# Second convolution of a pair placed behind the first of the next pair, and sixteen images as two written-out halves

## The chip, the core and the metric

The kernel runs on one core of one Trainium2 chip. The metric is the device time of one execution in microseconds (us), median of the runs shown. The core has five engines that run their own instruction streams and meet at semaphores: TensorE (PE, matmuls), VectorE (DVE), ScalarE (ACT), GpSimd (POOL) and SyncE (SP), which here only issues DMAs, in order.

## The reference, cut to what matters

Sixteen images of 64 channels and 64x64 pixels, float32. All sizes that the kernel works on follow from this:

```
# layer 0
y = leaky_relu(conv2d_3x3(x, conv_w1, conv_b1))
y = leaky_relu(conv2d_3x3(y, conv_w2, conv_b2))
seq = mamba(y as [16, 4096 tokens, 64], ...)      # state scan over 4096 tokens, 128 channels x 16 states
# layer 1, x = result of layer 0
out_c = channel attention(x)                      # 64x64 scores, softmax
out_s = softmax(q k^T over 4096x4096 tokens) v    # q, k of 32 channels
return x + w_bn @ concat(out_c, out_s)
```

The second convolution of an image needs the whole result of its first one, row by row with one row of overlap. The images are independent of each other everywhere.

## The kernel before, in words

There are two phases with barriers between.

**The convolutions** (`convolutions`, line 267). Images go in 8 pairs. A convolution of a pair is 8 chunks of 512 pixels, made as 4 "duos" of two chunks; a duo is 24 matmuls (lines 369 and 376) into two of the 8 PSUM banks. ACT adds the bias (line 388) and DVE makes the leaky ReLU: after the first convolution it writes into `ypad` (lines 404 and 407), after the second into `seq` (line 414). The 3x3 taps want a second copy of each image on the other 64 partitions, shifted by one row. For the input the copy is a second load (lines 313 and 314, into `xpad`); for the first convolution's result it is a DMA from `ypad` to `ypad` (lines 335 and 337, the "moves"). Both tiles exist twice, for even and odd pairs. The order on every engine is pair by pair: first convolution, then second. SP's order in a pair is: 16 loads of the next pair's input, 16 moves of this pair, 8 stores of `seq`. PE waits before a duo of the first convolution for its loads (`loaded`) and before a duo of the second for the moves of the chunks that it reads (`moved`):

```
for k in ((0, 1, 2) if j == 0 else range(2 * j + 1, min(2 * j + 3, CHUNKS))):
    pe.wait_ge(moved[par][k], 32 * (p // 2 + 1))
```

**The pipeline** (`pipeline`, line 419). Time is cut in ticks, 128 to an image and 16 to a chunk. In one tick all stages of several images are worked on: the scan of the current image (DVE line 1152, POOL line 1269, fed by the `lanes` DMAs of line 720 three ticks ahead), and the attention of the image before (PE lines 899, 901, 911, 926 and 836; ACT line 1007). `Span(j, images, tail)` lays out the ticks of consecutive images, and `span(...)` writes them out as one block of straight code per engine. A span begins at a tick where the neighbouring images' work is half done, so nothing of the computation is drained or repeated at a joint between spans. But the block ends: SP waits until every DMA of the span has landed (line 813), the engines meet at a barrier (line 264), GpSimd clears all semaphores one by one (line 263), and a second barrier follows. The spans are images 0 to 2 written out, then a hardware loop of three rounds with four images written out in its body (images 3 to 6, 7 to 10, 11 to 14), then image 15. That makes four joints: into the loop, two at its back edge, and out of it. In the loop the image number is a register, from which SP makes the DRAM addresses.

Of the kernel before, what the change touches and what calls it, by code (L numbers as in the profile page):

```python
# [23 lines left out]
P = 128  # L24
IMAGES, CH, HH, WW = 16, 64, 64, 64
L = HH * WW
PAIRS = IMAGES // 2
# [23 lines left out]
SEARCH = -6  # L51
TURN = SEARCH + KT + 1
QUERY_LOAD = SEARCH - 3
LOOPED = 4
END = 14
KEY_LOAD = [MAIN - KT + 8 * (p + 1) + 1 for p in range(QUARTERS)]
SEARCH_LOAD = [SEARCH - KT + 8 * (p + 1) + 1 for p in range(QUARTERS - 1)] + [GROUPS]
# [17 lines left out]
PAIRED = CHUNKS // 2  # L75


SPANS = ((0, 3, 0), (3, LOOPED, 0), (IMAGES - 1, 1, MAIN + TICKS + END + 1))
assert (IMAGES - 1 - 3) % LOOPED == 0 and NT * PAIRED == KT


def shape_constants():
# [181 lines left out]
    nc.all_engine_barrier()  # L264


def convolutions(nc, banks, x, w1, b1, w2, b2, seq_d):


# [2 lines left out]
    with ExitStack() as ctx:  # L272
# [20 lines left out]
        with nc.Block() as block:  # L293
# [10 lines left out]
            @block.sync  # L304
            def _(sp):
                def load_pair(p):

                    par = p % 2
                    for j in range(DUOS):
                        a, b = ROWS_OF[j:j + 2]  # L310
                        for i in range(2):
                            img = x[p, CH * i:CH * (i + 1), a:b, :]
                            sp.dma_start(xpad[par][i][0:CH, 1 + a:1 + b, 1:1 + WW], img).then_inc(loaded[par][j], 16)
                            sp.dma_start(xpad[par][i][CH:P, a:b, 1:1 + WW], img).then_inc(loaded[par][j], 16)

                for t, w, b, col in ((wtap[0], w1, b1, 0), (wtap[1], w2, b2, 1)):
                    sp.dma_start(t[0:CH, 0:3, :], w[:, 0:3, :]).then_inc(weights, 16)
                    sp.dma_start(t[CH:P, 0:3, :], w[:, 3:6, :]).then_inc(weights, 16)
                    for half in (0, CH):
                        sp.dma_start(t[half:half + CH, 3:6, :], w[:, 6:9, :]).then_inc(weights, 16)  # L320
                        sp.dma_start(bias[half:half + CH, col:col + 1], b).then_inc(weights, 16)
                sp.wait_ge(edged, 2)
                load_pair(0)
                for p in range(PAIRS):
                    par = p % 2
                    if p + 1 < PAIRS:
                        if p == 0:
                            sp.wait_ge(edged, 8)
                        else:
                            sp.wait_ge(summed, 2 * DUOS * (p - 1) + DUOS)  # L330
                        load_pair(p + 1)
                    for k in range(CHUNKS):
                        sp.wait_ge(leaky, 2 * CHUNKS * p + k + 1)
                        low, high = slice(1 + k * ROWS, 1 + (k + 1) * ROWS), slice(k * ROWS, (k + 1) * ROWS)
                        sp.dma_start(ypad[par][0][CH:P, high, 1:1 + WW],
                                     ypad[par][0][0:CH, low, 1:1 + WW]).then_inc(moved[par][k], 16)
                        sp.dma_start(ypad[par][1][0:CH, low, 1:1 + WW],
                                     ypad[par][1][CH:P, high, 1:1 + WW]).then_inc(moved[par][k], 16)
                    for k in range(CHUNKS):
                        sp.wait_ge(leaky, 2 * CHUNKS * p + CHUNKS + k + 1)  # L340
                        sp.dma_start(seq_d[2 * p:2 * p + 2].rearrange("a c l -> (a c) l")
                                     [:, k * CHUNK:(k + 1) * CHUNK], seq[:, k % 2, :]).then_inc(stored[k % 2], 16)
                for s in stored:
                    sp.wait_ge(s, 16 * PAIRS * CHUNKS // 2)

            @block.tensor
            def _(pe):
                pe.wait_ge(weights, 12 * 16)
                for p in range(PAIRS):
                    par = p % 2  # L350
                    for conv in range(2):
                        src = (xpad, ypad)[conv][par]
                        for j in range(DUOS):
                            first = 2 * CHUNKS * p + CHUNKS * conv + 2 * j
                            if first >= 8:
                                pe.wait_ge(plus_bias, first - 6)
                            if conv:

                                for k in ((0, 1, 2) if j == 0 else range(2 * j + 1, min(2 * j + 3, CHUNKS))):
                                    pe.wait_ge(moved[par][k], 32 * (p // 2 + 1))  # L360
                            else:
                                pe.wait_ge(loaded[par][j], 64 * (p // 2 + 1))
                            into = [[banks[(first + h) % 8][CH * i:CH * (i + 1), :].rearrange("p (h w) -> p h w", w=WW)
                                     for i in range(2)] for h in range(2)]
                            for h in range(2):
                                top = (2 * j + h) * ROWS
                                for dx in range(3):
                                    for i in range(2):
                                        nc.tensor.matmul(into[h][i], wtap[conv][:, dx, :],
                                                         src[i][:, top:top + ROWS, dx:dx + WW],  # L370
                                                         start=dx == 0, stop=False)
                            for dx in range(3):
                                for h in range(2):
                                    o, top = CH * h, (2 * j + h) * ROWS + 2 - h
                                    for i in range(2):
                                        mm = nc.tensor.matmul(into[h][i], wtap[conv][o:o + CH, 3 + dx, :],  # L376
                                                              src[i][o:o + CH, top:top + ROWS, dx:dx + WW],
                                                              start=False, stop=dx == 2, tile_position=(o, CH * i))
                            mm.then_inc(summed, 1)

            @block.scalar
            def _(act):
                for n in range(2 * CHUNKS * PAIRS):
                    conv = n // CHUNKS % 2
                    act.wait_ge(summed, n // 2 + 1)
                    if n >= 2:
                        act.wait_ge(leaky, n - 1)
                    nc.scalar.activation(biased[:, n % 2, :], banks[n % 8][:], ACT.Identity,  # L388
                                         bias=bias[:, conv:conv + 1]).then_inc(plus_bias, 1)

            @block.vector
            def _(dve):
                dve.wait_ge(edged, 8)
                for p in range(PAIRS):
                    y0, y1 = ypad[p % 2]
                    for n in range(2 * CHUNKS):
                        conv, k = n // CHUNKS, n % CHUNKS
                        dve.wait_ge(plus_bias, 2 * CHUNKS * p + n + 1)
                        src = biased[:, n % 2, :]
                        if conv == 0:  # L400
                            if p >= 2 and k == 0:
                                dve.wait_ge(summed, 2 * DUOS * (p - 1))
                            src = src.rearrange("p (h w) -> p h w", w=WW)
                            nc.vector.scalar_tensor_tensor(
                                out=y0[0:CH, 1 + k * ROWS:1 + (k + 1) * ROWS, 1:1 + WW], in0=src[0:CH],
                                scalar=LEAK, in1=src[0:CH], op0=ALU.mult, op1=ALU.max)
                            nc.vector.scalar_tensor_tensor(
                                out=y1[CH:P, k * ROWS:(k + 1) * ROWS, 1:1 + WW], in0=src[CH:P],
                                scalar=LEAK, in1=src[CH:P], op0=ALU.mult, op1=ALU.max).then_inc(leaky, 1)
                        else:  # L410
                            before = (CHUNKS * p + k) // 2
                            if before:
                                dve.wait_ge(stored[k % 2], 16 * before)
                            nc.vector.scalar_tensor_tensor(out=seq[:, k % 2, :], in0=src, scalar=LEAK, in1=src,
                                                           op0=ALU.mult, op1=ALU.max).then_inc(leaky, 1)
# [3 lines left out]
def pipeline(nc, banks, seq_d, scratch, w_in, cw, cb, w_dt_t, w_dt, dt_b, w_bc, a_log, skip,  # L419
# [4 lines left out]
    with ExitStack() as ctx:  # L424
# [857 lines left out]
                            nc.gpsimd.tensor_tensor(usp[:], dsp[:], u[:, c % 2, :], ALU.mult).then_inc(S["du_in"], 1)  # L1282
            clear(nc, list(S.values()))

        span(*SPANS[0], 0)
        with nc.Fori(SPANS[1][0], IMAGES - LOOPED, LOOPED) as i:
            span(*SPANS[1], i)
        span(*SPANS[2], IMAGES - 1)


# [38 lines left out]
```

## Time and profile before

| | |
|---|---|
| time, median of 3 runs | 8423.08 us (8422.37 to 8431.92) |
| the profiled execution's own time | 8432.17 us |
| its span, first to last instruction | 8430.3 us |
| PE, DVE, ACT, POOL busy | 7658.1, 6758.3, 5963.6, 3407.8 us |
| convolution phase, first to last matmul | 17.9 to 585.7 us |
| first scan of image 0, last scan | 638.9 and 7957.4 us |

The convolution phase is 7% of the span. In the pipeline an image takes about 459 us where there is no joint. The time after the last scan is the attention of the last image.

In the rows below, "PE L369 MATMUL ... x24" is a run of matmul records of one line (a float32 matmul has two records). "[13.87 <-DMA ypad<-ypad]" is the engine's idle time ahead and what ended it.

### The profile page before, as it was taken

The page shows a single profiled execution, that of the slowest core. Times are in us where ns is not written, and L with a number is a line of the kernel's source. Part 1 is how long each engine was busy: PE and PEld are TensorE (multiplying, and loading weights), DVE is VectorE, ACT ScalarE, POOL GpSimd, SP SyncE. Part 2 cuts the span into 40 slices and gives each one's busy share as a digit, 9 for nine tenths or more (in the row PEclk, how much of TensorE's full clock was granted, in tenths as well). Part 3 has the DMA queues.
Part 4 walks back from the last instruction along what each step waited for, and adds up shares of the span by engine and source line. Part 5 has one row for each costly group of instructions (what it writes and reads, how often), then busy time and mean ns, then how long its engine had stood idle before and what let it go on. Part 6 is the DMA issues. An engine that isn't in the chain of part 4 may idle for free. (4 is left out here: it accounts for less than half of the span.)

```text
span 8430.3 us, 156342 instructions
## 1 busy us (share of the span) xinstructions
PE 7658.1 (91%) x48454; PEld 2321.5 (28%) x48454; DVE 6758.3 (80%) x10982; ACT 5963.6 (71%) x10582; POOL 3407.8 (40%) x4135
## 2 busy tenths in 40 slices
PE   8982389998999999989999999989999999989999
PEld 2220122222222222222222222222222222222222
DVE  2228889898989899888989898988989898989721
ACT  1114468777778788777877787877878787878754
POOL 0005544444444444444444444444444444434300
PEclk9985689999999999999999999999999999999999
DMA  8738878787787887877777878878787878778600
GB/s 130 121 80 217 216 202 202 196 200 186 195 206 193 201 202 197 197 190 195 197 196 198 207 191 201 200 181 201 200 201 196 201 192 206 197 183 202 150 26 11
DMA packets 886565, 1531.37 MB, mean 182 GB/s; under 512 B 409480, under 2 KB 459472, under 8 KB 885712
## 3 DMA queue, kind: packets, MB, share of 16 engines
q1 hardware_dynamic: 882640, 1520.79, 74.0%
q8 instruction: 389, 6.37, 0.4%
q14 instruction: 464, 3.80, 0.2%
q10 hardware_dynamic: 3072, 0.40, 0.0%
HBM read 1326.69 MB, written 176.95 MB: 178 GB/s over the span
## 5 line engine op out<-in xcount | busy, mean ns | idle before, releaser
L1269 POOL TENSOR_TENSOR hst<-hst,cbc 128x512 f32<-128x512 f32 x2048 | 2609.8, 1274 | 3664.6 <-DVE bank L1141 3642.7
L1152 DVE TENSOR_TENSOR_SCAN hst<-dA,carry,bank 128x512 f32<-128x512 f32 x1792 | 2293.8, 1280 | 94.7 <-ACT dA L1013 22.5
L1007 ACT ACTIVATE pr<-bank 128x512 f32<-128x512 f32 x4096 | 2226.6, 603 | 61.3 <-PE bank L901 59.1
L911 PE MATMUL bank<-pr,vt 128*32 128x512 f32 x16384 | 2192.5, 607 | 0.0
L952 ACT ACTIVATE gains<-bank 128x512 f32<-128x512 f32 x2048 | 1223.8, 598 | 1141.0 <-PE bank L836 748.8
L836 PE MATMUL bank<-s1kx,s1q 128*128 128x512 bf16 x4096 | 1588.2, 389 | 199.7 <-DMA s1kx<-kx_d 76.9
L1013 ACT ACTIVATE dA<-lanes,small 128x512 f32<-128x512 f32 x2048 | 1501.0, 733 | 354.7 <-DMA lanes<-spread_d 312.1
L899 PE MATMUL bank<-s1q,s1k 128*128 128x512 bf16 x4096 | 1568.2, 383 | 176.1 <-ACT pr L1007 152.5
L1141 DVE TENSOR_TENSOR bank<-lanes,bbc 128x512 f32<-128x512 f32 x2048 | 1514.9, 740 | 163.2 <-DMA lanes<-spread_d 56.7
L1093 DVE CUSTOM_DVE_ANT_0 gains<-bank,gains 128x512 f32<-128x512 f32 x2048 | 1369.7, 669 | 326.6 <-PE bank L836 319.2
L901 PE MATMUL bank<-t2q,t2k 128*128 128x512 bf16 x4096 | 1562.1, 381 | 0.0
L926 PE MATMUL bank<-pr,ones 128*32 128x512 f32 x8192 | 1069.5, 594 | 1.9 <-ACT dens L1022 1.7
L836 PEld LDWEIGHTS bank<-s1kx,s1q 128*128 128x128 bf16 x4096 | 397.6, 97 | 1779.5 <-issue 1137.0
L899 PEld LDWEIGHTS bank<-s1q,s1k 128*128 128x128 bf16 x4096 | 400.1, 98 | 710.1 <-ACT pr L1007 333.0
L873 PE MATMUL bank<-hst,cst 128*32 128x512 f32 x4096 | 484.4, 615 | 79.0 <-POOL hst L1269 79.0
L911 PEld LDWEIGHTS bank<-pr,vt 128*32 128x32 f32 x16384 | 323.7, 108 | 789.8 <-issue 777.4
L901 PEld LDWEIGHTS bank<-t2q,t2k 128*128 128x128 bf16 x4096 | 403.0, 98 | 403.4 <-issue 10.6
L1262 POOL COPY carry<-hst 128x1 f32<-128x1 f32 x1792 | 483.8, 270 | 40.3 <-DVE hst L1152 35.8
L926 PEld LDWEIGHTS bank<-pr,ones 128*32 128x32 f32 x8192 | 266.5, 111 | 626.2 <-issue 522.1
L388 ACT ACTIVATE biased<-bank,bias 128x512 f32<-128x512 f32 x128 | 80.9, 683 | 504.0 <-PE bank L376 504.0
L1133 DVE SCALAR_TENSOR_TENSOR ysb<-u,small,bank 128x512 f32<-128x512 f32 x128 | 95.6, 747 | 340.8 <-issue 324.7
L1152 DVE TENSOR_TENSOR_SCAN hst<-dA,bank 128x512 f32<-128x512 f32 x256 | 312.4, 1220 | 15.2 <-ACT dA L1013 5.4
(116 smaller groups left out, 5720.7 us busy)
## 6 DMA issues: line engine op xcount, KB each, us to landing
lanes<-spread_d SPq DMA_DIRECT2D x2048, 512.0 KB, 6.0
seqt<-seq_d SPq DMA_DIRECT2D x256, 128.0 KB, 4.5
spread_d<-dsp SPq DMA_DIRECT2D x128, 256.0 KB, 2.0
spread_d<-usp SPq DMA_DIRECT2D x128, 256.0 KB, 2.0
bbc<-bc_d SPq DMA_DIRECT2D x128, 256.0 KB, 3.7
cbc<-bc_d SPq DMA_DIRECT2D x128, 256.0 KB, 4.2
xpad<-in_x SPq DMA_DIRECT2D x64, 256.0 KB, 6.8
ypad<-ypad SPq DMA_DIRECT2D x128, 128.0 KB, 4.2
```

Source lines behind the costliest of these rows:

```text
L836: mm = nc.tensor.matmul(bank[:].rearrange("p (c n) -> p c n", n=HALF), s1q[:, q, nt * P:(nt + 1) * P], keys[:, 2 * mc:2 * (mc + 1), 1 if k ...
L899: nc.tensor.matmul(bank[:], s1k[:, t * P:(t + 1) * P], s1q[:, q, cols], start=True, stop=False)
L901: nc.tensor.matmul(bank[:], t2k[:, t * P:(t + 1) * P], t2q[:, q, cols], start=False, stop=True).then_inc(S["ring_full"], 1)
L911: mm = nc.tensor.matmul(ACC[CH * h + o:CH * h + o + BLOCK, :], vt[:, t, o:o + BLOCK], pr[:, T % PRING, h, :], start=t == 0, stop=t == KT - ...
L926: mm = nc.tensor.matmul(DEN[o:o + 32, :], ones[:], pr[:, (2 * p + par) % PRING, h, :], start=t == 1, stop=t == KT - 1, tile_position=(0, o))
L952: nc.scalar.activation(gains[:, k % 2, :], bank_of(e)[:], ACT.Relu).then_inc(S["act_took"], 1)
L1007: nc.scalar.activation(pr[:, T % PRING, h, :], bank_of(("S", T, h))[:], ACT.Exp).then_inc(S["p_full"], 1)
L1013: nc.scalar.activation(dA[:, (T + 1) % 2, :], lanes[:, (T + 1) % SLOTS, 0, :], ACT.Exp, scale=amat[:, g:g + 1]).then_inc(S["da_in"], 1)
L1093: nc.vector.tensor_tensor_reduce(out=gains[:, k % 2, :], in0=bank[:], in1=gains[:, k % 2, :], scale=1.0, scalar=LOWEST, op0=ALU.add, op1=A ...
L1141: nc.vector.tensor_tensor(DBU[:], lanes[:, T % SLOTS, 1, :], bbc[:, sl % 2, :], ALU.mult).then_inc(S["dbu_in"], 1)
L1152: nc.vector.tensor_tensor_scan(hst[:, slot_of(T), :], dA[:, T % 2, :], DBU[:], carry[:, g:g + 1] if sl % CHUNKS else 0.0, ALU.mult, ALU.ad ...
L1269: nc.gpsimd.tensor_tensor(h, h, cbc[:, (T - 1) // GROUPS % 2, :], ALU.mult).then_inc(S["hc_in"], 1)
```

## The change

It has two parts. In `convolutions`, a list `STAGES` gives the order of (pair, convolution): (0,0), (1,0), (0,1), (2,0), (1,1), ... (7,0), (6,1), (7,1). All engines and SP's queue run over this list; the semaphore counts are recomputed from the place in it. Which buffers there are, and each instruction, stay as they were.

In `pipeline`, the spans are two: images 0 to 7 and images 8 to 15, both written out, with the one joint between. The hardware loop and its register are gone.

```diff
-SPANS = ((0, 3, 0), (3, LOOPED, 0), (IMAGES - 1, 1, MAIN + TICKS + END + 1))
+SPANS = ((0, IMAGES // 2, 0), (IMAGES // 2, IMAGES // 2, MAIN + TICKS + END + 1))
...
+STAGES = [(0, 0)] + [e for p in range(1, PAIRS) for e in ((p, 0), (p - 1, 1))] + [(PAIRS - 1, 1)]
+STAGE_OF = {e: s for s, e in enumerate(STAGES)}
...
-                for p in range(PAIRS):
+                for s, (p, conv) in enumerate(STAGES):
                     par = p % 2
-                    if p + 1 < PAIRS:
-                        if p == 0:
-                            sp.wait_ge(edged, 8)
-                        else:
-                            sp.wait_ge(summed, 2 * DUOS * (p - 1) + DUOS)
-                        load_pair(p + 1)
...
+                    if conv == 0:
+                        if p + 1 < PAIRS:
+                            if p == 0:
+                                sp.wait_ge(edged, 8)
+                            else:
+                                sp.wait_ge(summed, DUOS * (STAGE_OF[p - 1, 0] + 1))
+                            load_pair(p + 1)
+                        for k in range(CHUNKS):
+                            sp.wait_ge(leaky, CHUNKS * s + k + 1)
...
+                    else:
+                        for k in range(CHUNKS):
+                            sp.wait_ge(leaky, CHUNKS * s + k + 1)
...
-                                dve.wait_ge(summed, 2 * DUOS * (p - 1))
+                                dve.wait_ge(summed, DUOS * (STAGE_OF[p - 2, 1] + 1))
...
-        span(*SPANS[0], 0)
-        with nc.Fori(SPANS[1][0], IMAGES - LOOPED, LOOPED) as i:
-            span(*SPANS[1], i)
-        span(*SPANS[2], IMAGES - 1)
+        for spread_over in SPANS:
+            span(*spread_over, spread_over[0])
```

PE behind the first convolution of pair 1. `xpad10` is the input tile of an odd pair, `ypad10` and `ypad00` the first convolution's results of an odd and an even pair. Before:

```order
L376 MATMUL bank7<-xpad10,w1tap 64x512
L376 MATMUL bank7<-xpad11,w1tap 64x512
L369 MATMUL bank0<-ypad10,w2tap 64x512
L369 MATMUL bank0<-ypad11,w2tap 64x512
L369 MATMUL bank0<-ypad10,w2tap 64x512
```

After:

```order
L380 MATMUL bank7<-xpad10,w1tap 64x512
L380 MATMUL bank7<-xpad11,w1tap 64x512
L373 MATMUL bank0<-ypad00,w2tap 64x512
L373 MATMUL bank0<-ypad01,w2tap 64x512
L373 MATMUL bank0<-ypad00,w2tap 64x512
```

Behind pair 1's first convolution PE read pair 1's own result, and now it reads pair 0's.

SP's queue at the end of the moves of pair 0. Before:

```order
L335 DMA ypad<-ypad 64x8x64
L337 DMA ypad<-ypad 64x8x64
L341 DMA seq_d<-seq 128x512 x8
L313 DMA xpad<-in_x 64x17x64
L314 DMA xpad<-in_x 64x17x64
```

After:

```order
L339 DMA ypad<-ypad 64x8x64
L341 DMA ypad<-ypad 64x8x64
L316 DMA xpad<-in_x 64x17x64
L317 DMA xpad<-in_x 64x17x64
L316 DMA xpad<-in_x 64x17x64
```

The eight stores of `seq` stood between the moves of pair 0 and the loads of pair 2; they now stand behind the moves of pair 1.

DVE at the end of the loop's body before (line 1286 is the back edge; `energy` is the last small piece of an image, and the scan without `carry` begins the next one):

```order
L1123 TENSOR_TENSOR energy<-energy,bank0 64x64
L1141 TENSOR_TENSOR bank5<-lanes,bbc 128x512
L1152 SCALAR_TENSOR_TENSOR hst<-dA,carry,bank5 128x512
L1093 ISA gains,mxp<-bank4,gains 128x512
L1093 ISA mxp 128x1
L654 UNCONDITIONAL_BRANCH
L1286 REGISTER_ALU
L1286 COMPARE_AND_BRANCH
L1072 UNCONDITIONAL_BRANCH
```

DVE at the one joint after:

```order
L1127 TENSOR_TENSOR energy<-energy,bank4 64x64
L1145 TENSOR_TENSOR bank5<-lanes,bbc 128x512
L1156 SCALAR_TENSOR_TENSOR hst<-dA,carry,bank5 128x512
L1097 ISA gains,mxp<-bank3,gains 128x512
L1097 ISA mxp 128x1
L658 UNCONDITIONAL_BRANCH
L1076 UNCONDITIONAL_BRANCH
L1145 TENSOR_TENSOR bank5<-lanes,bbc 128x512
```

The joint that stays has the block's two branches and no compare of a loop register. At the other fourteen borders between images no branch stands.

## Rows read from the trace of the kernel before

**Rows 1.** The page's first line.

```profile
span 8430.3 us, 156342 instructions
```

**Rows 2.** Waits, 0 to 600 us: waiter, releaser, total, times, longest.

```profile
PE bank L369 <- DMA ypad<-ypad: 37.5, 7, 13.9
```

**Rows 3.** Timeline of PE in the convolutions: start, duration, what, idle before.

```profile
17.93 7.80 PE L369 MATMUL bank<-xpad,w1tap 128*64 128x512 f32 x24 [17.93 <-DMA xpad<-in_x]
...
28.41 5.37 PE L369 MATMUL bank<-xpad,w1tap 128*64 128x512 f32 x24
...
36.45 5.37 PE L369 MATMUL bank<-xpad,w1tap 128*64 128x512 f32 x24
...
66.47 7.43 PE L369 MATMUL bank<-ypad,w2tap 128*64 128x512 f32 x24 [13.87 <-DMA ypad<-ypad]
...
582.86 2.81 PE L376 MATMUL bank<-ypad,w2tap 64*64 64x512 f32 x24
```

**Rows 4.** Timeline of SP's queue in the convolutions: issue start, duration.

```profile
55.34 1.29 SPq L314 DMA_DIRECT2D xpad<-in_x  x1
...
383.56 0.63 SPq L313 DMA_DIRECT2D xpad<-in_x  x1
...
407.49 1.47 SPq L335 DMA_DIRECT2D ypad<-ypad  x1
...
420.45 0.64 SPq L337 DMA_DIRECT2D ypad<-ypad  x1
```

**Rows 5.** Tile `xpad`: time from issue to landing of its DMAs.

```profile
DMA to landing us min/median/max: 4.0/6.6/8.1
```

**Rows 6.** Windows: stretch, length, busy per engine, granted clock, DMA share, GB/s.

```profile
510.00:540.00 30.00, 30.00 (x186) 9.04 (x184) 7.08 (x11) 5.06 (x8) 0.00 (x0) 1.00 0.19 56
...
2401.50:3319.70 918.20, 880.08 (x5674) 267.18 (x5672) 825.05 (x1349) 732.56 (x1308) 421.92 (x512) 0.99 0.80 199
```

**Rows 7.** Timeline of DVE: the first scans of images 2, 4, 6, 8, 10, 12, 14, 15.

```profile
1470.19 1.22 DVE L1152 TENSOR_TENSOR_SCAN hst<-dA,bank 128x512 f32<-128x512 f32 x1
...
2401.51 1.22 DVE L1152 TENSOR_TENSOR_SCAN hst<-dA,bank 128x512 f32<-128x512 f32 x1
...
3319.66 1.22 DVE L1152 TENSOR_TENSOR_SCAN hst<-dA,bank 128x512 f32<-128x512 f32 x1
...
4258.23 1.22 DVE L1152 TENSOR_TENSOR_SCAN hst<-dA,bank 128x512 f32<-128x512 f32 x1
...
5176.01 1.22 DVE L1152 TENSOR_TENSOR_SCAN hst<-dA,bank 128x512 f32<-128x512 f32 x1
...
6112.19 1.22 DVE L1152 TENSOR_TENSOR_SCAN hst<-dA,bank 128x512 f32<-128x512 f32 x1
...
7030.52 1.22 DVE L1152 TENSOR_TENSOR_SCAN hst<-dA,bank 128x512 f32<-128x512 f32 x1
...
7502.61 1.22 DVE L1152 TENSOR_TENSOR_SCAN hst<-dA,bank 128x512 f32<-128x512 f32 x1
```

**Rows 8.** Timeline of DVE: tick 112 of image 2, ticks 32 and 112 of 4, 32 of 15.

```profile
1873.21 1.28 DVE L1152 TENSOR_TENSOR_SCAN hst<-dA,carry,bank 128x512 f32<-128x512 f32 x1
...
2522.07 1.28 DVE L1152 TENSOR_TENSOR_SCAN hst<-dA,carry,bank 128x512 f32<-128x512 f32 x1
...
2804.86 1.28 DVE L1152 TENSOR_TENSOR_SCAN hst<-dA,carry,bank 128x512 f32<-128x512 f32 x1
...
7624.92 1.28 DVE L1152 TENSOR_TENSOR_SCAN hst<-dA,carry,bank 128x512 f32<-128x512 f32 x1
```

**Rows 9.** Timeline of DVE: its first instruction behind each of the four joints.

```profile
1940.09 0.70 DVE L1141 TENSOR_TENSOR bank<-lanes,bbc 128x512 f32<-128x512 f32 x1 [11.22 <-PEq L264]
...
3795.67 0.70 DVE L1141 TENSOR_TENSOR bank<-lanes,bbc 128x512 f32<-128x512 f32 x1 [16.05 <-issue]
...
5649.57 0.70 DVE L1141 TENSOR_TENSOR bank<-lanes,bbc 128x512 f32<-128x512 f32 x1 [14.24 <-issue]
...
7501.87 0.70 DVE L1141 TENSOR_TENSOR bank<-lanes,bbc 128x512 f32<-128x512 f32 x1 [12.71 <-PEq L264]
```

More of the change, by code:

```diff
@@ L53 @@
 QUERY_LOAD = SEARCH - 3
-LOOPED = 4
 END = 14
@@ L75 @@
 PAIRED = CHUNKS // 2
-SPANS = ((0, 3, 0), (3, LOOPED, 0), (IMAGES - 1, 1, MAIN + TICKS + END + 1))
-assert (IMAGES - 1 - 3) % LOOPED == 0 and NT * PAIRED == KT
+SPANS = ((0, IMAGES // 2, 0), (IMAGES // 2, IMAGES // 2, MAIN + TICKS + END + 1))
+assert NT * PAIRED == KT
 def shape_constants():
@@ L323, in _ @@
                 load_pair(0)
-                for p in range(PAIRS):
+                for s, (p, conv) in enumerate(STAGES):
                     par = p % 2
-                    if p + 1 < PAIRS:
-                        if p == 0:
-                            sp.wait_ge(edged, 8)
-                        else:
-                            sp.wait_ge(summed, 2 * DUOS * (p - 1) + DUOS)
-                        load_pair(p + 1)
[L332 to L342, printed above, removed]
@@ new lines, in _ @@
+                    if conv == 0:
[7 more added lines that the diff above has]
+                            sp.wait_ge(leaky, CHUNKS * s + k + 1)
+                            low, high = slice(1 + k * ROWS, 1 + (k + 1) * ROWS), slice(k * ROWS, (k + 1) * ROWS)
+                            sp.dma_start(ypad[par][0][CH:P, high, 1:1 + WW],
+                                         ypad[par][0][0:CH, low, 1:1 + WW]).then_inc(moved[par][k], 16)
+                            sp.dma_start(ypad[par][1][0:CH, low, 1:1 + WW],
+                                         ypad[par][1][CH:P, high, 1:1 + WW]).then_inc(moved[par][k], 16)
+                    else:
+                        for k in range(CHUNKS):
+                            sp.wait_ge(leaky, CHUNKS * s + k + 1)
+                            sp.dma_start(seq_d[2 * p:2 * p + 2].rearrange("a c l -> (a c) l")
+                                         [:, k * CHUNK:(k + 1) * CHUNK], seq[:, k % 2, :]).then_inc(stored[k % 2], 16)
@@ L348, in _ @@
                 pe.wait_ge(weights, 12 * 16)
-                for p in range(PAIRS):
+                for s, (p, conv) in enumerate(STAGES):
                     par = p % 2
[L351 to L364, printed above, removed]
-                            for h in range(2):
[L366 to L379, printed above, removed]
@@ new lines, in _ @@
+                    src = (xpad, ypad)[conv][par]
+                    for j in range(DUOS):
+                        first = CHUNKS * s + 2 * j
+                        if first >= 8:
+                            pe.wait_ge(plus_bias, first - 6)
+                        if conv:
+                            for k in ((0, 1, 2) if j == 0 else range(2 * j + 1, min(2 * j + 3, CHUNKS))):
+                                pe.wait_ge(moved[par][k], 32 * (p // 2 + 1))
+                        else:
+                            pe.wait_ge(loaded[par][j], 64 * (p // 2 + 1))
+                        into = [[banks[(first + h) % 8][CH * i:CH * (i + 1), :].rearrange("p (h w) -> p h w", w=WW)
+                                 for i in range(2)] for h in range(2)]
+                        for h in range(2):
+                            top = (2 * j + h) * ROWS
+                            for dx in range(3):
+                                for i in range(2):
+                                    nc.tensor.matmul(into[h][i], wtap[conv][:, dx, :],
+                                                     src[i][:, top:top + ROWS, dx:dx + WW],
+                                                     start=dx == 0, stop=False)
+                        for dx in range(3):
+                            for h in range(2):
+                                o, top = CH * h, (2 * j + h) * ROWS + 2 - h
+                                for i in range(2):
+                                    mm = nc.tensor.matmul(into[h][i], wtap[conv][o:o + CH, 3 + dx, :],
+                                                          src[i][o:o + CH, top:top + ROWS, dx:dx + WW],
+                                                          start=False, stop=dx == 2, tile_position=(o, CH * i))
+                        mm.then_inc(summed, 1)
@@ L383, in _ @@
                 for n in range(2 * CHUNKS * PAIRS):
-                    conv = n // CHUNKS % 2
+                    conv = STAGES[n // CHUNKS][1]
                     act.wait_ge(summed, n // 2 + 1)
@@ L393, in _ @@
                 dve.wait_ge(edged, 8)
-                for p in range(PAIRS):
+                for s, (p, conv) in enumerate(STAGES):
                     y0, y1 = ypad[p % 2]
-                    for n in range(2 * CHUNKS):
-                        conv, k = n // CHUNKS, n % CHUNKS
-                        dve.wait_ge(plus_bias, 2 * CHUNKS * p + n + 1)
+                    for k in range(CHUNKS):
+                        n = CHUNKS * s + k
+                        dve.wait_ge(plus_bias, n + 1)
                         src = biased[:, n % 2, :]
```

## The prediction, made before the changed kernel was run

> **What bounds the kernel now.** I read the page first, then the waits and PE's timeline of the convolutions, then SP's queue there, then the first scan of each image in DVE's timeline, and last what stands behind each joint. The span is 8430.3 us [rows 1], and the profiled execution took 8432.17 us in all, 1.9 more. The reader is to see three things.
>
> First, in the convolutions PE is the bound. Two successive duos start at 28.41 and 36.45 [rows 3], so a duo takes 8.04 us, and over 30 us in the last pair PE is busy for all of them at granted clock 1.00 [rows 6]. But seven times, once in each pair but the last, it waits for the moves of `ypad`, 37.5 us together, 13.9 in the first pair [rows 2] and so about 3.9 in each other. Behind such a wait it starts slowly: the first 24 matmul records took 7.43 us at 66.47, and 5.37 where PE had come without a gap [rows 3].
>
> Second, why it waits is in SP's queue: the 16 loads of the next pair are issued from 383.56 to 407, and only then the moves, 407.49 to 421.1 [rows 4], though their data were there long before. In the last pair there is nothing to load, and no wait.
>
> Third, in the pipeline the joints show. Images 4 and 5, with no joint, take 3319.66 - 2401.51 = 918.15 us, 459.1 each. Images 2 and 3 with the first joint between them take 931.32, 6 and 7 with the first back edge 938.57, 10 and 11 with the second 936.18, and image 14, up to behind the last joint, 472.09 [rows 7].
>
> **Part one, the convolutions.** From the first to the last matmul PE spends 582.86 + 2.81 - 17.93 = 567.74 us [rows 3]. There are 64 duos, 64 x 8.04 = 514.6. The very first starts slowly in either kernel, 10.48 instead of 8.04, so 2.4 more: 517.0. What is left, 50.7, is the seven waits with 37.5 [rows 2] and 13.2 of slow starts behind them, about 2 us each. All of it goes if no wait takes their place. What could:
>
> - Loads. In the new order SP issues the loads of pair p+1 as stage (p,0) starts, and PE wants them two stages later, behind (p-1,1). A stage is 4 duos, 32.2 us, so 64 us after. The 16 issues take 24 us [rows 4] and the last lands at most 8.1 us later [rows 5]: 32 us to spare. The start is tighter, since PE now wants pair 1 directly behind pair 0: first duo at 17.93 + 10.48 + 3 x 8.04 = 52.5, fourth at 76.7. The last load of pair 1 is issued until 56.63 [rows 4] and lands by 64.7, 12 us early. The four loads of the first duo stand 12 issues before that one, at 1.5 us each some 18 us, so they are issued by about 39 and land by 47, some 5 us early; this is the smallest cushion.
> - Moves. They still stand behind the loads and end 421.1 - 383.6 = 37.5 us after these began. PE wants them 64 us after the loads began. 27 us to spare.
> - Stores of `seq`. They now queue behind the moves. Counted from the start of the loads, stage (p-1,1) begins at 32.2 us, its first duo is through ACT and DVE some 10 us later, at 42, and SP is free at 37.5. In stage (0,1) alone SP is late: it is still at pair 2's loads and pair 1's moves until about 70 + 37.5 = 108, and the stores of chunks 0 and 1, ready at 95, wait 13 us. DVE's third chunk then waits for its buffer. Behind DVE stands ACT (two `biased` buffers), behind ACT PE, but PE may run six chunks ahead, 24 us. No cost.
> - The reuse of `ypad`. DVE may write pair p's result once (p-2,1) is done, and that is the stage directly before (p,0) on PE; DVE's first chunk comes 8 us into it. No wait.
>
> From both sides: the part is worth 37.5 if every slow start stays elsewhere, and 50.7 if all goes. The least would be the six small waits coming back as waits for loads, about 24 of the 37.5. Nothing there can be won beyond 50.7, since PE is then without a gap. I take 50.7; the last pair, which had no load in front of it, is the row nearest to this state.
>
> **Part two, the joints.** Against 918.15 for two images the first joint costs 13.2 us, the first back edge 20.4, the second 18.0 [rows 7]. The last costs 472.09 - 459.1 = 13.0 in image 14 and something behind it: the first 32 ticks of image 15 take 122.31 us, those of image 4 120.56 [rows 8], so 1.8; 14.8 together. All four: 66.4. Most of it is the standstill, in which DVE does nothing for 11.22, 16.05, 14.24 and 12.71 us [rows 9]; the rest is the run-up, again at the low clock. One joint stays. It has no loop on either side, so I price it at the lower two, 13.2 (first) to 14.8 (last), and take 13.2. 66.4 - 13.2 = 53.2 us go.
>
> At the two back edges the standstill is longer than at the other two joints: (16.05 + 14.24)/2 against (11.22 + 12.71)/2 is 15.1 against 12.0, so 3.2 us more each [rows 9]. The Trainium skill, "Runtime: NRT & Kernel Launch", Instruction fetch mechanics, says that instructions stream in sequentially and that a taken branch to a place outside the window held makes the engine fetch before it goes on. By that rule the excess belongs to the branch back and is gone for good. If the joints merely scattered, the one that stays would cost the mean of the four, 66.4/4 = 16.6, and 49.8 would go instead of 53.2.
>
> Does an image written out run as fast as one in the loop? Image 2 was written out already. Its first 112 ticks take 1873.21 - 1470.19 = 403.02, those of image 4, in the loop, 2804.86 - 2401.51 = 403.35 [rows 7, 8]. So nothing for the register arithmetic of SP that goes, and nothing for straight code twice as long. From both sides: by these rows 0.3 us per image gained, 4 us over the 12 images that were in the loop, or scatter of the same size as loss.
>
> **The sum.** 50.7 + 53.2 = 103.9. 8432.17 - 103.9 = 8328.3 by the profiled execution's own time. That execution is 9.1 us above the median shown, 8423.08; the runs shown lie at 8422, 8423 and 8432, so such a time is not rare. By the median the sum is 8319.2. I take 8322, between the two and nearer the median's.
>
> **The rivals.**
>
> *A wait takes part of the convolutions' gain.* Moves or loads land later when PE no longer pauses, because the same bytes now go in a shorter time. For it: 16 issues of loads take 24 us [rows 4], so SP's queue itself is slowed, and a pair's time falls from about 71 to 64 us. Against it: 27 and 32 us to spare. It would leave about 24 us of waits and their slow starts: 8322 + 25 to 35, about 8350.
>
> *The joint in the middle costs more.* It has eight images' instructions behind it and must start a far piece of code. For it: joints differ by 7 us with what follows them. Against it: entering the loop was itself a jump into new code and was the cheapest. 5 to 7 us more: 8328.
>
> *The whole thing is slower: TensorE's clock.* The convolutions now run 517 us without one pause. If the granted clock fell from its upper level, 2.4 GHz, to the lower, 1.2 GHz, under this, each further duo would cost 8.04 us more; from 13 duos at the low level the gain of 103.9 is used up, and if the second half of the phase ran so, 32 duos, the time would be 8322 + 257 = 8579. Against it: the rows have 1.00 in the last pair, without a gap for about 98 us, and 0.99 over 918 us of the pipeline with PE busy for 880 of them [rows 6].
>
> *The reordering does nothing.* PE would meet the same waits if SP's queue still served each move late. Then only the joints are won: 8322 + 50.7 = 8373. Against it: the moves' deadline moved by a full stage and the queue's work did not.
>
> **How the numbers follow.** Forecast as worked out: 0.76, its own range 8311 to 8334. Dearer joint: 0.08, 8328, within it nearly. Part of the waits back: 0.07, 8350. Reordering without effect: 0.03, 8373. Slower by the clock or by some supply of instructions that the rows do not show: 0.03. The last 0.03 is a gain larger than worked out. For 8 in 10 I take 8309 to 8338: the low end is the median's sum less 4 for the images and 6 for scatter, the high end the profiled execution's sum and 10 more, as for a dearer joint with some of the waits. A change of 0.2%, 17 us, is about what can be told from no change here. All cases but the slow one gain over 17 us. So faster 0.95, the same 0.02, slower 0.03.
>
> **What would show it.** In the changed kernel's profile: PE's waits for `ypad` moves gone from the list, and none for `xpad` beyond the first; first to last matmul of the convolutions 517 us; 24 records in 5.37 us everywhere but at the start; one joint, with DVE still for 11 to 13 us ahead of image 8; image periods 459 at all other borders. It is wrong if `xpad` waits appear in stage (1,0), if the first scan of image 0 comes later than 590, or if two images without a joint take more than 920 us.

## The result and the profile after

The changed kernel took 8324.12 us, median of 4 runs (8321.60 to 8334.52), the kernel before 8427.45 in the same comparison (8422.37 to 8431.92). The ratio is 0.988, 95% interval 0.9865 to 0.9894. The profiled execution was the slowest of the four, 8334.52 us. On another chip, in a later set of runs, the two stood at 8331.05 and 8430.1, ratio 0.9881 (0.9866 to 0.9896). The forecast was 8322.

The page's first line and instruction-fetch queues of the changed kernel, against [rows 1]:

```profile
span 8332.7 us, 153459 instructions
...
q8 instruction: 385, 6.31, 0.4%
q14 instruction: 428, 3.51, 0.2%
```

Nearly 2,900 instructions fewer were executed, those of the loop and its addresses. The written-out code is about twice as long, yet less of it was fetched: in the page of before the last two lines had 389 and 464 packets, 6.37 and 3.80 MB.

PE's timeline in the convolutions of the changed kernel, its first run of matmuls and its last, answering to [rows 3]:

```profile
17.66 7.09 PE L373 MATMUL bank<-xpad,w1tap 128*64 128x512 f32 x24 [17.66 <-DMA xpad<-in_x]
...
531.23 2.81 PE L380 MATMUL bank<-ypad,w2tap 64*64 64x512 f32 x24
```

PE's waits in the first 600 us of the changed kernel (waiter, releaser, total, times, longest). The waits for `ypad` of [rows 2] are gone, and the only one for `xpad` is the first load:

```profile
PE bank L541 <- DMA dA<-in_w_bn_t: 18.7, 1, 18.7
PE bank L373 <- DMA xpad<-in_x: 17.7, 1, 17.7
PE bank L862 <- DVE u L1185: 5.7, 1, 5.7
PE bank L858 <- DMA seqt<-seq_d: 5.1, 1, 5.1
```

The stretch from the first to the last convolution matmul is 531.23 + 2.81 - 17.66 = 516.4 us, where it was 567.7. The window over it (length, busy of PE, PEld, DVE, ACT, POOL, granted clock, DMA share, GB/s):

```profile
17.90:535.00 517.10, 516.13 (x3072) 156.47 (x3070) 128.41 (x191) 80.61 (x128) 0.00 (x0) 1.00 0.79 127
```

PE is busy for all of it at granted clock 1.00, and the same bytes now take 0.79 of the DMA engines' time.

DVE's timeline at the one joint, then the first scans of images 4, 6, 7 and 9, answering to [rows 9] and [rows 7]:

```profile
4189.01 0.70 DVE L1145 TENSOR_TENSOR bank<-lanes,bbc 128x512 f32<-128x512 f32 x1 [11.50 <-PEq L263]
```

```profile
2337.81 1.22 DVE L1156 TENSOR_TENSOR_SCAN hst<-dA,bank 128x512 f32<-128x512 f32 x1
...
3259.32 1.22 DVE L1156 TENSOR_TENSOR_SCAN hst<-dA,bank 128x512 f32<-128x512 f32 x1
...
3717.26 1.22 DVE L1156 TENSOR_TENSOR_SCAN hst<-dA,bank 128x512 f32<-128x512 f32 x1
...
4650.65 1.22 DVE L1156 TENSOR_TENSOR_SCAN hst<-dA,bank 128x512 f32<-128x512 f32 x1
```

Images 7 and 8 with the joint between take 933.4 us, images 4 and 5 without one 921.5. The latter were 918.15 before, and the prediction had named more than 920 for two images without a joint as a sign that it is wrong. In the second trace of the changed kernel they take 920.9. What this says of the prediction is taken up below.

For the comparisons below, this table gives of each profiled execution the stretch of the convolutions (first to last matmul) and the stretch from the first scan of image 0 to the last scan of image 15, both read from the timelines as above.

| kernel | joints | convolutions | scans |
|---|---|---|---|
| before | 4, 2 of them back edges | 567.7 | 7318.6 |
| changed, two executions | 1 | 516.4, 517.4 | 7272.2, 7266.7 |
| convolutions alone | 4, 2 of them back edges | 516.2 | 7316.7 |
| halves alone | 1 | 566.6 | 7265.6 |
| old stages, moves first | 1 | 517.1 | 7266.6 |
| five written-out spans | 4 | 516.4 | 7310.3 |
| one span, two executions | 0 | 517.4, 517.5 | 7262.7, 7263.2 |
| eight spans | 7 | 517.0 | 7345.0 |
| eight spans, clears dealt out | 7 | 516.4 | 7323.5 |
| one span, SEARCH -5 | 0 | 517.5 | 7199.8 |
| one span, SEARCH -4 | 0 | 516.9 | 7463.9 |

The tail behind the last scan was 469 to 473 us in all of them.

### The profile page after: what moved, and what is told of

The parts are those of the page before. It is cut to its first block, busy times and chain, and to the rows that moved or that the text cites. A ratio compares the mean times of both kernels' runs of the same rounds, so it can differ in the third digit from the quotient of the medians.

```text
span 8332.7 us, 153459 instructions
## 1 busy us (share of the span) xinstructions
PE 7638.9 (92%) x48454; PEld 2320.1 (28%) x48454; DVE 6757.6 (81%) x10982; ACT 5962.3 (72%) x10582; POOL 3408.2 (41%) x4135
## 4 chain that ended last, share of the span: by engine, by line
PE 42%; ACT 3%; issue 2%; DMA 1%; ACTq 1%; DVE 1%; SPq 0%; DVEq 0%
PE bank L915 12%; PE bank L840 6%; PE bank L930 6%; PE bank L903 5%; PE bank L905 5%; PE bank L877 3%; ACT L1011 1%; ACT gains L956 1%; PE bank L885 1%; PE bank L872 1%; PE bank L862 1%; ACT pr L1011 1%; PE bank L858 1%; ACTq L1033 1%; DMA s1kx<-kx_d 1%
## 5 line engine op out<-in xcount | busy, mean ns | idle before, releaser
L1011 ACT ACTIVATE pr<-bank 128x512 f32<-128x512 f32 x4096 | 2226.7, 603 | 59.4 <-PE bank L905 57.7
```

The lines of the kernel that those rows point to most:

```text
L1011: nc.scalar.activation(pr[:, T % PRING, h, :], bank_of(("S", T, h))[:], ACT.Exp).then_inc(S["p_full"], 1)
```

## The experiments

**Each part alone.** The new order of the convolutions with the old spans and loop:

```diff
-SPANS = ((0, IMAGES // 2, 0), (IMAGES // 2, IMAGES // 2, MAIN + TICKS + END + 1))
+SPANS = ((0, 3, 0), (3, LOOPED, 0), (IMAGES - 1, 1, MAIN + TICKS + END + 1))
...
-        for spread_over in SPANS:
-            span(*spread_over, spread_over[0])
+        span(*SPANS[0], 0)
+        with nc.Fori(SPANS[1][0], IMAGES - LOOPED, LOOPED) as i:
+            span(*SPANS[1], i)
+        span(*SPANS[2], IMAGES - 1)
```

> The new order of the convolutions alone; spans and loop as before. Theory: the two parts are independent and this one is worth 50 to 51 us, so about 51 us under the kernel before and about 52 above the changed one (8376 where these have 8427 and 8324); PE from first to last convolution matmul in about 516 us, with no wait but the first. Rival: PE without pauses is worth less than the standstill that went (waits move to the start of the pipeline, whose first loads then come earlier): under 40 us.

Measured: 8379.56 us (8376.0 to 8381.4), the kernel before 8427.84 (8417.4 to 8440.3) on the same chip; ratio 0.9942 (0.9928 to 0.9955). That is 48.3 less by the medians and 51.5 by the stretch in the traces; the scans kept their length within 2 us. The theory holds, and the rival's 40 is excluded by the trace: the first scan comes 53.2 us behind the last convolution matmul in both kernels, so no wait moved to the start of the pipeline.

The halves alone, with the convolutions in the old order, is the other half of the diff:

> The two written-out halves alone; convolutions in the old order. Theory as predicted: 53 us under the kernel before (8374). Rival, from the changed kernel's trace, where the stretch from the first to the last scan became only 46.3 us shorter: images written out cost about 0.6 us more each, and this part is worth 46 us (8381). Convolutions 568 us, waits for ypad moves of 37 us.

Measured: 8382.08 us (8378.7 to 8388.5), ratio 0.9947 (0.9934 to 0.9961): 45.8 less by the medians, 53.0 by the scans in the trace. The kernel before scatters over 23 us in these runs, so the medians do not decide between 46 and 53. The traces of four executions with this layout (changed kernel twice, this one, and the one with moves first) have 7272.2, 7266.7, 7265.6 and 7266.6: 46.4 to 53.0 less than the trace of before, and 44.5 to 51.1 less than the trace of the convolutions alone, which has the old joints too. So 53 is the upper end of what was measured, not its middle. The two parts alone add up to 94.1 us by the medians; together they gave 103.3 and 99.1. The waits for `ypad` here:

```profile
PE bank L369 <- DMA ypad<-ypad: 36.0, 7, 13.1
```

**Why PE waited: the stage order or SP's queue.** Here the stages stay in the old order, and only the block with the wait and `load_pair(p + 1)` goes behind the moves:

```diff
-                    if p + 1 < PAIRS:
-                        if p == 0:
-                            sp.wait_ge(edged, 8)
-                        else:
-                            sp.wait_ge(summed, 2 * DUOS * (p - 1) + DUOS)
-                        load_pair(p + 1)
                     for k in range(CHUNKS):
                         sp.wait_ge(leaky, 2 * CHUNKS * p + k + 1)
...
+                    if p + 1 < PAIRS:
+                        if p == 0:
+                            sp.wait_ge(edged, 8)
+                        else:
+                            sp.wait_ge(summed, 2 * DUOS * (p - 1) + DUOS)
+                        load_pair(p + 1)
```

> The old stage order (both convolutions of a pair in a row) in the two written-out halves, with SP's 16 loads of the next pair moved behind its 16 moves. Theory: PE waited for the moves only since they stood behind the loads in SP's queue, so this wins the same 50 us as the new stage order: the convolutions in 516 to 518 us, the time that of the changed kernel within 2 us. Rival 1: the new stage order is needed, because moves of the last chunks land after PE wants them: seven waits of 1 to 3 us stay, and the time is 10 to 35 us above the changed kernel. Rival 2: the loads, now issued about 32 us later, come too late for the next pair: waits for xpad appear.

Measured: 8329.14 us (8327.7 to 8330.2), the changed kernel on the same chip 8331.05 (8328.2 to 8331.5). PE's only slow piece in the convolutions is again the first, and its last matmuls end at 535.20:

```profile
18.15 7.76 PE L369 MATMUL bank<-xpad,w1tap 128*64 128x512 f32 x24 [18.15 <-DMA xpad<-in_x]
...
532.39 2.81 PE L376 MATMUL bank<-ypad,w2tap 64*64 64x512 f32 x24
```

So the whole 50 us are had without the new order. The cause of the waits was the place of the moves in SP's queue, and both rivals fall. But this kernel has less to spare. The loads now stand in front of the stores of `seq`, DVE waits for these 23 times, and ACT stands behind DVE (in all, times, longest):

```profile
DVE seq L414 <- DMA seq_d<-seq: 193.9, 23, 24.3
ACT biased L388 <- DVE seq L414: 148.4, 23, 17.8
```

In the changed kernel DVE's wait for the stores was 23.0 us in 4 times. PE has no such wait in either; it may run ahead into the other banks.

**The joints without a loop.** `SPANS = ((0, 3, 0), (3, 4, 0), (7, 4, 0), (11, 4, 0), (IMAGES - 1, 1, MAIN + TICKS + END + 1))` in the changed kernel.

> New order of the convolutions; joints at the same four places as before (ahead of images 3, 7, 11, 15), but all written out, no hardware loop. Theory: a joint without a jump back costs 13 to 15 us wherever it stands, so this is the changed kernel plus 3 x 13 to 15 = 39 to 45 us (about 8366), and 10 to 12 us under the kernel with the new convolutions and the loop. Rival: joints merely scatter between 13 and 20 us; then this equals that kernel (8376).

Measured: 8372.0 us (8371.0 to 8373.5), 6 above the 8366 expected. That is 7.6 under the kernel with the new convolutions and the loop on the same chip, so 3.8 per back edge. DVE's standstill ahead of image 7 in this kernel:

```profile
3743.09 0.70 DVE L1145 TENSOR_TENSOR bank<-lanes,bbc 128x512 f32<-128x512 f32 x1 [11.92 <-PEq L263]
```

and at the same place, a back edge, in the kernel with the new convolutions and the loop:

```profile
3741.57 0.70 DVE L1146 TENSOR_TENSOR bank<-lanes,bbc 128x512 f32<-128x512 f32 x1 [15.62 <-issue]
```

It is 3.7 longer. At the second back edge, ahead of image 11, it is 3.6 longer (14.84 against 11.27), and at the joints into and out of the loop it is not clearly so (12.10 and 11.64 against 12.22 and 10.67). The scatter theory falls; the excess of a back edge is real but smaller than the 10 to 12 us for two that were expected.

What fills it can be read from the trace of the kernel before. Behind the clears and the barrier the engines come to the loop's compare-and-branch at 3791.96 to 3792.10. The register arithmetic in front of it takes 0.05 us, the branch itself lasts 4.2 us on PE, and SP goes on at 3795.32. The DMA queues in this stretch (3792:3796) carry nothing but instructions:

```profile
q14 instruction: 7, 0.06, 4.4%
q8 instruction: 1, 0.02, 2.9%
```

The first five of these packets begin 0.8 to 1.2 us behind the branch, and the largest lasts 1.9 us. At the same joint written out, from 3738 to 3744 in the kernel with five spans, there is no packet of any queue. So the excess lies in the branch, and what moves meanwhile is code; the arithmetic is not it.

**No joint.** `SPANS = ((0, IMAGES, MAIN + TICKS + END + 1),)`.

> The changed kernel with all sixteen images in one span, no joint at all. Theory: one joint less, 13 us under the changed kernel (8311). Rival 1: more straight code costs something per image, and nothing or less than 5 us is gained. Rival 2: the standstill also lets queues catch up, so the image behind it is faster and the gain is less than 10.

Measured: 8320.18 us (8316.1 to 8325.4), ratio to before 0.9870 (0.9855 to 0.9885). Against the four written-out joints on the same chip it is 51.8 less, 13.0 per joint (47.6 and 11.9 by the scans). Against the changed kernel, on another chip, only 4, where 13 were expected: this does not decide between the theory and its rivals.

The changed kernel and the one-span kernel once more:

> The changed kernel once more, on the same chip as the three below. Four joints written out came 51.8 us above none, 13.0 each, so theory: this kernel lies 13 us above the one without a joint (8320), at 8333. Rival: the single joint in the middle is worth only the 4 us that the first medians say (8324 against 8320).

> All sixteen images in one span, once more, beside the two below. Against the changed kernel's 8331 on the chip of the second call, and 8324 on the first, theory says 13 us less for the joint: 8311 to 8318. It says nothing new if it comes out at 8320 as before, since the chips differ by as much.

Measured: 8331.05 us (8328.2 to 8331.5) against its 8430.1 of before, and 8322.06 (8318.1 to 8325.9) against its 8437.82, so 99.1 and 115.8 less. The changed kernel came within 2 us of the 8333 expected, and the one-span kernel above the 8311 to 8318 expected for it. The two were never on the same chip, and the difference comes out between 2 and 17 us depending on what it is taken against. The scans in the traces say 3.5 to 9.5, or down to 2.4 with the other two kernels of the changed kernel's layout.

**Many joints.** `SPANS = tuple((2 * n, 2, 0) for n in range(7)) + ((IMAGES - 2, 2, MAIN + TICKS + END + 1),)`.

> Eight spans of two images each, all written out: seven joints instead of one, otherwise the changed kernel. Theory: 6 x 13.0 = 78 us above the changed kernel of the same call. Rival, that joints give back part of their cost in the images behind them, and the more so the nearer they stand: 6 x 10 or less, under 60 us.

Measured: 8412.48 us (8408.8 to 8419.6), 81.4 above the changed kernel on the same chip, 13.6 per joint (78.3 and 13.1 by the scans). The theory holds; joints every two images give nothing back.

In the same kernel the clears are dealt out:

```diff
-    for s in sems:
-        nc.gpsimd.sem_clear(s)
+    for n, s in enumerate(sems):
+        (nc.gpsimd, nc.sync, nc.scalar, nc.vector)[n % 4].sem_clear(s)
     nc.all_engine_barrier()
```

> The same seven joints, with the clearing of the semaphores dealt out in turn to GpSimd, SP, ACT and DVE. In the changed kernel's joint GpSimd stands 5.3 us over 74 clears, 0.07 us each. Theory: this piece is in series with everything, and three quarters of it, 4.0 us per joint, go: 28 us under the kernel with seven joints. Rival: the standstill is set by SP's wait for the last stores and by the lanes that must come again, and the clears lie beside those: under 5 us in all.

Measured: 8384.25 us (8380.2 to 8393.8), 28.2 less, as expected, but not all of it in the joints. DVE's first instruction of image 8, with all clears on GpSimd and with them dealt out:

```profile
4222.86 0.70 DVE L1145 TENSOR_TENSOR bank<-lanes,bbc 128x512 f32<-128x512 f32 x1 [10.77 <-PEq L263]
```

```profile
4207.40 0.70 DVE L1145 TENSOR_TENSOR bank<-lanes,bbc 128x512 f32<-128x512 f32 x1 [7.24 <-PEq L263]
```

The standstill is 3.5 us shorter. The trace has the clears themselves: a span clears 71 semaphores, not the 74 of the expectation, in 5.0 to 5.3 us when GpSimd does all, and in 1.5 to 1.8 when four engines share them. The edit acts at ten places: the seven joints, the end of the last span, and twice between the convolutions and the pipeline, where 37 more are cleared (2.9 us, then 0.8). Eight times 3.5 and these 2 are 30 us, of which 28.2 came. The theory's 4.0 at seven places gave the right sum with the wrong share: the scans, which hold the joints alone, became 21.5 us shorter, 3.1 per joint. The clears are in series with everything. Two windows of the changed kernel's joint show the rest:

```profile
4176.80:4183.00 6.20, 0.34 (x4) 0.00 (x0) 0.71 (x3) 0.55 (x1) 0.22 (x1) 0.92 0.41 122
4183.00:4189.00 6.00, 0.00 (x0) 0.02 (x1) 0.00 (x0) 0.00 (x0) 0.00 (x0) 0.50 0.01 1
```

For about 6 us the last DMAs land while the engines have nothing left, and for 6 more nothing moves but the clears and barriers. In these the granted clock is at the lower level, 1.2 GHz, at which PE then begins.

**A version that beats both.** In the one-span trace PE stands for the last quarter of `s1kx` once in nearly every image (in all, times, longest):

```profile
PE bank L840 <- DMA s1kx<-kx_d: 85.1, 15, 7.7
```

`SEARCH` is the tick at which the next image's search for row maxima begins. The edit is `SEARCH = -5`, then `-4`, in the one-span kernel.

> One span, and the search for the row maxima of the next image one tick later (SEARCH -5 instead of -6). In the one-span trace PE stands 5.6 us once per image for the last quarter of s1kx and then runs at the low clock; the second chunk of an image takes 64 us, the others 56.5. Theory: this stall is a DMA latency that starts when the last piece of the image before is stored, so a tick (3.5 us) more between store and use takes 3 us or more off each image, and the slow start where the stall falls to nothing: 45 to 90 us in all. Rival: the stall is the channel attention's chain in the same tick, or moves to the row maxima's other end (the four queries' rows come a tick later): under 15 us, or slower.

> The same with two ticks later (SEARCH -4). Theory: the stall is gone, 90 to 120 us under the one-span kernel. Rival as for one tick; here the maxima come only two ticks before the first scores of the quarter need them, so a new wait for their rows (ACT's small DMAs) may show in ticks 30 to 32 of each quarter, 64 times, and eat 1 us each.

Measured: 8257.80 us with -5 (8253.9 to 8267.9), ratio to before 0.9789 (0.9775 to 0.9802), and 8529.66 with -4 (8514.9 to 8533.5), ratio 1.0107 (1.0092 to 1.0122). Against the one-span kernel on the same chip that is 64.3 less, within the 45 to 90 expected, and 207.6 more. PE's waits with -5:

```profile
PE bank L903 <- DMA t2q<-nm: 83.6, 56, 2.9
...
PE bank L840 <- DMA s1kx<-kx_d: 1.2, 1, 1.2
```

and with -4:

```profile
PE bank L903 <- DMA t2q<-nm: 252.1, 58, 7.0
```

One tick takes the stall of `s1kx` away, 85.1 to 1.2 us, and already brings in the wait for the rows of maxima, 1.5 us in each of 56 quarters. These two waits are of the same total, so they alone do not explain a gain. Two more things show in the traces of the one-span kernel and of this one from the same chip. PE's waits for `mxp` and `gains` fall from 75.3 to 27.6 us (lines 840 and 903), and PE is busy 24.6 us less for the same matmuls, so fewer of them ran at the low clock. Seen by chunks (16 ticks), the second chunk of an image falls from 64.3 to 57.2 us, and the four chunks in which a quarter begins rise by 0.7 to 1.2 each. The second tick has no stall left to win and makes the new wait 4.3 us each; those four chunks take 60.7 to 62.2 us. The theory for -4 was wrong in sign: the new wait was named, with 1 us each, but it is four times that, and it comes 58 times where the stall came 15 times.

## Why the prediction was right

The convolutions' term was 50.7. The stretch shrank by 51.4, since the very first duo also started 0.7 us faster, and by 50.4 in the second trace, where it did not; with the part alone it was 51.5. The cushions sufficed: no wait for loads or moves came, though that does not measure each of them. One was smaller than worked out: SP came to pair 2's loads only at 70.77 us, behind the moves of pair 0, and PE wanted them at 115.86, so 45 us later and not 64; the last was issued by 95.4, still in time. Even the cost-free delay in stage (0,1) is there. SP's first store, which the prediction put at 108 us, and DVE's third chunk behind it:

```profile
108.16 13.12 SPq L346 DMA_DIRECT2D seq_d<-seq  x8
```

```profile
112.14 1.29 DVE L418 SCALAR_TENSOR_TENSOR seq<-biased 128x512 f32<-128x512 f32 x2 [18.25 <-DMA seq_d<-seq]
```

DVE stands 18 us, and PE, which may run ahead into the eight banks, does not.

What the prediction did not see is that the same gain needed no new stage order. It named SP's queue as the reason and still priced the new order as the cure; the moves-first kernel shows that the queue alone was it.

The joints' term was 53.2. It measured 46.4 in the first trace and 51.9 to 53.0 in three others of the same layout, and 45.8 by the medians of the part alone. Its direction and reason are right, but that it came so near is in part luck: it is a difference of two prices that were both too high. All four old joints were set at 66.4. Between the kernel without a joint and the two with the old joints the scans differ by 53.5 to 55.9 us, and the medians by 59.4. The joint that stays was set at 13.2, and against none it measured 2.4 to 9.5 in the scans. Both prices were taken against two images of one trace, and these were faster than the images of a kernel without a joint.

Inside the four, the excess of a back edge over a plain joint was set at about 5 us (20.4 and 18.0 against 13.2 and 14.8) and measured 3.8. The five written-out spans show that it goes with the loop, and the trace shows the fetch behind the branch. The Trainium skill, "Runtime: NRT & Kernel Launch", Instruction fetch mechanics, says that a taken branch to a place outside the window held makes the engine fetch before it goes on. The trace agrees, with the 4.2 us branch on PE and the instruction packets behind it. The price of a plain joint, 13.2, is near the 13.0 and 13.6 (11.9 and 13.1 by the scans) where several are compared on one chip.

"Written-out images cost nothing" holds only within the scatter of a trace: from image 2 on, images without a joint and not right behind one take 457 to 462 us, looped or not. Yet one named sign of being wrong did come, images 4 and 5 with 921.5 us against the limit of 920. It was set 2 us above a single reading of 918.15, tighter than such pairs scatter, and the theory does not fall with it; but it points at the term for written-out images, which was put at nothing and is where the open end below lies.

Of the rivals, the slow clock is excluded by the window at 1.00 over 517 us, the return of waits by the list of waits, and the reordering without effect by the convolutions alone. "The joint in the middle costs more" is not borne out: its standstill was 11.50 us, at the low end of [rows 9], and images 7 and 8 took 11.9 us more than 4 and 5.

The sum against the profiled execution's own time was 8328.3, measured 8334.5; against the median 8319.2, measured 8324.1. The taking of a place between the two was a hedge. Both are 5 to 6 us short. For the profiled execution this is the 7 us by which the scans of the first trace shrank less than 53.2. For the median it is mostly the starting point: the sum began at 8423.08, and the kernel before stood at 8427.45 beside the changed one, so the gain itself was 103.3 where 103.9 was forecast.

What stays open is the price of the last joint. Several joints cost 13 to 14 each in the medians, but one against none comes out at 2 to 9 us in the scans. Images 2 to 14 of the one-span kernel average 459.9 and 459.7 us in its two traces, against 459.0 for those away from joints in the kernel before and 459.2 to 459.7 in those with two halves; whether long runs without a standstill run a little slower or traces scatter so was not settled.

## What to carry to other kernels

A wait that appears on a compute engine may be a place in a queue: look at what the DMA queue issues ahead of the awaited transfer, and move that first, before reordering the computation. A barrier between pieces of straight code is a sum of parts in series (last stores landing, clears, refill, low clock); compare the period with and without it over whole iterations, then price the parts with a kernel that has many, and count every place at which an edit acts before dividing. A stage moved by one step wins until the next deadline binds, and if that one comes more often, one step further loses more than all was won.

## What the runs showed of the hardware

Clearing one semaphore takes 0.07 us on GpSimd (71 in 5.3 us), and dealing 71 of them to four engines shortened the standstill by 3.5 us (10.77 to 7.24). A jump back cost 3.8 us more than going on into written-out code, and in this time the trace has the branch (4.2 us on PE) and packets of instructions. In the written-out code no image from image 2 on that has no joint in it or right before it took over 462 us, so no stall of fetching shows; whether less than 1 us per image hides there is open. The median of the kernel before was 8423 to 8438 us in different sets of runs, so that parts of 5 us could be told only between kernels on the same chip, or in the stretches of the traces.
